# First experts of a two-layer mixture-of-experts kernel: output products as three products of split operands, written-out loop, two gather buffers

## The reference, cut to what matters

```python
B, L, D = (4, 1024, 256); F = 1024; E = 16        # here 2 x 1024 tokens, so capacity = 128
_, idx = jax.lax.top_k(logits.T, top_k)            # each expert takes its 128 best tokens
xe = xn[idx]
h = jnp.einsum('ecd,efd->ecf', xe, fc1_weight) + fc1_bias[:, None, :]
h = jax.nn.gelu(h, approximate=False)
y = jnp.einsum('ecf,edf->ecd', h, fc2_weight) + fc2_bias[:, None, :]
gates = jnp.take_along_axis(probs.T, idx, axis=1)
contrib = (y * gates[:, :, None]).reshape(-1, d)
output = jnp.zeros((n_tokens, d), dtype=x.dtype).at[flat_idx].add(contrib)
gate_sums = jnp.zeros((n_tokens, 1), dtype=x.dtype).at[flat_idx].add(gates.reshape(-1, 1))
```

## Time and profile before

| what | value |
|---|---|
| time of the kernel before, median of 3 runs | 859.65 us (858.2 to 859.97) |
| the profiled execution's own time | 855.36 us |
| its span on the core | 853.6 us |
| mean granted TensorE clock, share of full speed | 0.877 |
| PE busy | 681.3 us (80%) |
| DVE / ACT / POOL busy | 477.6 / 341.7 / 401.6 us |
| stage of the first experts, first transpose to last scatter's issue | 233.4 to 358.8 us |

### The profile page before, as it was taken

One profiled execution on the slowest core, in us unless ns is written; L12 is line 12 of the kernel. 1 busy time (PEld: TensorE's weight loads), 2 busy tenths in 40 slices (PEclk: granted clock), 3 DMA queues, 4 the chain that ended last, 5 costly groups with the idle time before them and its releaser, 6 DMA issues. The chain is left out here.

```text
span 853.6 us, 14267 instructions
## 1 busy us (share of the span) xinstructions
PE 681.3 (80%) x4385; PEld 624.7 (73%) x4386; DVE 477.6 (56%) x1023; ACT 341.7 (40%) x739; POOL 401.6 (47%) x515
## 2 busy tenths in 40 slices
PE   0767777710599999669999998996999999999980
PEld 0666667600499989656888877886899899999980
DVE  3353554368511111163988788974677864676740
ACT  1243435210033323224333343324766665667750
POOL 2132112000144455432565556643687766887883
PEclk9767585555699999869999999997999999999995
DMA  8961490040059998289010102007676564572221
GB/s 235 146 166 39 111 338 0 6 121 4 7 171 322 314 314 231 39 288 332 13 38 26 38 26 76 13 5 238 207 221 200 141 187 87 171 207 40 41 48 21
DMA packets 91760, 111.56 MB, mean 131 GB/s; under 512 B 9632, under 2 KB 80672, under 8 KB 91296
## 3 DMA queue, kind: packets, MB, share of 16 engines
q1 hardware_dynamic: 74032, 89.66, 34.4%
q0 software_dynamic: 11536, 14.30, 9.1%
q10 hardware_dynamic: 6112, 6.61, 2.3%
HBM read 93.84 MB, written 17.32 MB: 130 GB/s over the span
## 5 line engine op out<-in xcount | busy, mean ns | idle before, releaser
L1939 POOL DMA_INDIRECT out<-nyg,si x51 | 82.2, 1611 | 17.9 <-issue 17.9
L1538 POOL TENSOR_TENSOR hidl<-sums,hidh 128x512 fp32r<-128x512 f32 x40 | 52.2, 1305 | 76.4 <-ACT hidh L1726 76.4
L121 POOL TENSOR_TENSOR held<-ones 128x1 f32<-128x1 f32 x137 | 44.8, 327 | 90.1 <-DMA acc<-myg,si 34.2
L1358 POOL DMA_INDIRECT nG<-ytab,gi x54 | 77.4, 1434 | 16.3 <-issue 16.2
L2051 ACT ACTIVATE nh<-npH,c_sb 128x288 f32<-128x288 f32 x128 | 63.5, 501 | 45.4 <-PE npH L1992 44.8
L1851 DVE SCALAR_TENSOR_TENSOR xc<-pY,W,xc 128x264 f32<-128x264 f32 x160 | 67.3, 484 | 0.0
L1611 PE MATMUL pU<-xparts,gparts 128*128 128x512 f32 x240 | 65.3, 408 | 1.3 <-DVE xparts L1782 1.3
L1611 PE MATMUL pG<-xparts,gparts 128*128 128x512 f32 x240 | 63.1, 398 | 1.7 <-ACT sums L1711 1.7
L1104 PEld LDWEIGHTS mpH<-mXT,w_sb 128*128 128x128 f32 x512 | 61.2, 196 | 1.8 <-DVE mXT L1135 1.1
L1104 PE MATMUL mpH<-mXT,w_sb 128*128 128x128 f32 x512 | 61.5, 280 | 0.7 <-DVE mXT L1135 0.7
L1622 PE MATMUL pY<-dparts,hidh 128*128 128x264 f32 x320 | 60.4, 284 | 0.0
(11 more groups left out here) (412 smaller groups left out, 1857.3 us busy)
## 6 DMA issues: line engine op xcount, KB each, us to landing
w_sb<-in_w SPq DMA_DIRECT2D x32, 1024.0 KB, 8.4
w_sb<-in_v SPq DMA_DIRECT2D x30, 1024.0 KB, 8.9
bias_sb<-in_bias SPq DMA_DIRECT2D x4, 1024.0 KB, 14.7
gw<-in_wgate SPq DMA_DIRECT2D x17, 128.0 KB, 2.2
gw<-in_wup SPq DMA_DIRECT2D x17, 128.0 KB, 2.4
acc<-zrow SPq DMA_DIRECT2D x1, 2056.0 KB, 25.6
sums<-acc SPq DMA_DIRECT2D x4, 514.0 KB, 5.7
x_sb<-in_x SPq DMA_DIRECT2D x1, 2048.0 KB, 10.8
```

The source lines that it names most:

```text
L121: pool.tensor_tensor(held[:, n:n + 1], ones[:, 0:1], ones[:, 0:1], ALU.mult)
L1358: pool.indirect_dma_start(G[:, n], None, ytab, bass.IndirectOffsetOnAxis(ap=gi3[:, n:n + 1], axis=0)).then_inc(gathered, 16)
L1538: pool.tensor_tensor(hidl[:, s % 2], hid[:, s % 2], hidh[:, s % 2], ALU.subtract).then_inc(lo_ready, 1)
L1939: pool.indirect_dma_start(result, bass.IndirectOffsetOnAxis(ap=si3[:, n:n + 1], axis=0), yg[:, n], None, bounds_check=B * N - 1, oob_is_er ...
```

## The change

The function is replaced by straight code for all 16 blocks, with no loop.

- The output products take split operands: ACT rounds the hidden values `hT` to `hh` and the expert's second weights to `w2high`; DVE forms the rests `hl` and `w2low`; PE makes 24 products of 256 columns in fp32r instead of 8 in fp32. The first products stay plain fp32.
- PE runs one block behind: `first(j+1)`, `turn(j+2)`, `second(j)`. The bank of first products `pH` is doubled, and so are the split operands.
- The gathered rows have two buffers, and POOL issues the gather of block j+3 ahead of the scatter of block j.
- SP reloads a buffer once the block's first products are done and its second weights are split (`w_low`), no longer after its output products.
- DVE's order within a block is: outputs of block j-1, `low` of expert j+1 (128x2048), `column` of block j+2, and the rests of block j+1's hidden values in two halves.
- The stage ends with a wait for its last scatter.

```diff
@@ -991,172 +991,187 @@
-            def expert_phase(tag, src, width, dst, out_width, gidx, sidx, gates, from_row, b1t, b2t, w1t, w2t,
-                             experts, act_fn, counts):
...
-                            with eng.Fori(0, experts // RING) as r:
-                                for u in range(RING):
...
-                                for c in range(FC):
-                                    pe.wait_ge(gelu_done, j * FC + c + 1)
-                                    ins = pe.matmul(pY[:, 0:D], hT[:, c], w2_sb[:, u, c], start=(c == 0), stop=(c == FC - 1))
-                                ins.then_inc(fc2_done, 1)
...
-            expert_phase("m", table[0:B * N, :], ROW, acc0, D + 1, idx, idx, gtab, True, b1_sb, b2_sb, w1, w2,
-                         E0, ACT.Gelu, None)
+                G = sb("mG", [P, 2, ROW], into=ph)
+                XT = sb("mXT", [P, KD, P], into=ph)
+                hT = sb("mhT", [P, FC, P], into=ph)
+                hh = sb("mhh", [P, 2, FC, P], F32R, into=ph)
+                hl = sb("mhl", [P, 2, FC, P], F32R, into=ph)
+                w2high = sb("mw2h", [P, 2, FC, D], F32R, into=ph)
+                w2low = sb("mw2l", [P, 2, FC, D], F32R, into=ph)
+                yt = sb("myt", [P, D], into=ph)
+                yg = sb("myg", [P, D + 1], into=ph)
+                pX = ps("mpX", [P, 512], ph)
+                pH = ps("mpH", [P, 2, 2, 512], ph)
+                pY = ps("mpY", [P, 512], ph)
...
+                    @block.sync
+                    def _(sp):
+                        for e in range(E0 - RING):
+                            sp.wait_ge(fc1_done, 2 * e + 2)
+                            sp.wait_ge(w_low, e + 1)
+                            load_expert(sp, w1, w2, e + RING, e % RING)
+                    @block.gpsimd
+                    def _(pool):
+                        def gather(j):
+                            if j >= 1:
+                                pool.wait_ge(gathered, 16 * j)
+                            if j >= 2:
+                                pool.wait_ge(turned, j - 1)
+                                pool.wait_ge(xt_ready, j - 1)
                                 held_here(pool, 1)
+                            pool.tensor_copy(gi[:], idx[:, j:j + 1]).then_inc(gi_set, 1)
+                            pool.wait_ge(gi_set, j + 1)
+                            held_here(pool, 0)
+                            pool.indirect_dma_start(G[:, j % 2], None, table[0:B * N, :],
+                                                    bass.IndirectOffsetOnAxis(ap=gi[:], axis=0)).then_inc(gathered, 16)
+                        for j in range(3):
+                            gather(j)
+                        for j in range(E0):
+                            if j + 3 < E0:
+                                gather(j + 3)
+                            if j >= 1:
+                                pool.wait_ge(scattered, 16 * j)
                                 held_here(pool, 2)
+                            pool.tensor_copy(si[:], idx[:, j:j + 1]).then_inc(si_set, 1)
+                            pool.wait_ge(yg_ready, j + 1)
+                            pool.wait_ge(si_set, j + 1)
+                            held_here(pool, 3)
+                            pool.indirect_dma_start(acc0, bass.IndirectOffsetOnAxis(ap=si[:], axis=0), yg[:], None,
+                                                    compute_op=ALU.add).then_inc(scattered, 16)
+                        pool.wait_ge(scattered, 16 * E0)
+                        held_here(pool, 2)
+                    @block.tensor
+                    def _(pe):
+                        def turn(j):
+                            pe.wait_ge(gathered, 16 * (j + 1))
+                            if j >= 1:
+                                pe.wait_ge(xt_ready, j)
+                            for k in range(KD):
+                                ins = pe.transpose(pX[:, k * P:(k + 1) * P], G[:, j % 2, k * P:(k + 1) * P], ident[:])
+                            ins.then_inc(turned, 1)
+                        def first(j):
+                            pe.wait_ge(xt_ready, j + 1)
+                            pe.wait_ge(w_in[j % RING], 32 * (j // RING + 1))
+                            if j >= 2:
+                                pe.wait_ge(gelu_done, 2 * (j - 1))
+                            for c in range(FC):
                                 for k in range(KD):
+                                    ins = pe.matmul(pH[:, j % 2, c // HC, (c % HC) * P:(c % HC + 1) * P],
+                                                    w1_sb[:, j % RING, k, c * P:(c + 1) * P], XT[:, k], start=(k == 0), stop=(k == KD - 1))
+                                if c % HC == HC - 1:
+                                    ins.then_inc(fc1_done, 1)
+                        def second(j):
+                            pe.wait_ge(w_low, j + 1)
+                            if j >= 1:
+                                pe.wait_ge(y_read, j)
+                            for c in range(FC):
+                                if c % HC == 0:
+                                    pe.wait_ge(hl_ready, 2 * j + c // HC + 1)
+                                pe.matmul(pY[:, 0:D], hl[:, j % 2, c], w2high[:, j % 2, c], start=(c == 0), stop=False)
+                                pe.matmul(pY[:, 0:D], hh[:, j % 2, c], w2low[:, j % 2, c], start=False, stop=False)
+                                ins = pe.matmul(pY[:, 0:D], hh[:, j % 2, c], w2high[:, j % 2, c], start=False, stop=(c == FC - 1))
+                            ins.then_inc(fc2_done, 1)
+                        turn(0)
+                        first(0)
+                        turn(1)
+                        for j in range(E0):
+                            if j + 1 < E0:
+                                first(j + 1)
+                            if j + 2 < E0:
+                                turn(j + 2)
+                            second(j)
+                    @block.scalar
+                    def _(act):
+                        def high(e):
+                            act.wait_ge(w_in[e % RING], 32 * (e // RING + 1))
+                            if e >= 2:
+                                act.wait_ge(fc2_done, e - 1)
+                            act.activation(w2high[:, e % 2], w2_sb[:, e % RING], ACT.Copy).then_inc(w_high, 1)
+                        def hidden(j):
+                            for half in range(2):
+                                act.wait_ge(fc1_done, 2 * j + half + 1)
+                                if j >= 1:
+                                    act.wait_ge(hl_ready, 2 * (j - 1) + half + 1)
+                                for c in range(HC * half, HC * half + HC):
+                                    ins = act.activation(hT[:, c], pH[:, j % 2, half, (c % HC) * P:(c % HC + 1) * P], ACT.Gelu,
+                                                         bias=b1_sb[:, j, c:c + 1])
+                                ins.then_inc(gelu_done, 1)
+                                act.wait_ge(gelu_done, 2 * j + half + 1)
+                                if j >= 2:
+                                    act.wait_ge(fc2_done, j - 1)
+                                cs = slice(HC * half, HC * half + HC)
+                                act.activation(hh[:, j % 2, cs], hT[:, cs], ACT.Copy).then_inc(hh_ready, 1)
+                        high(0)
+                        hidden(0)
+                        for j in range(E0):
+                            if j + 1 < E0:
+                                high(j + 1)
+                                hidden(j + 1)
+                    @block.vector
+                    def _(dve):
+                        def column(j):
+                            dve.wait_ge(turned, j + 1)
+                            if j >= 1:
+                                dve.wait_ge(fc1_done, 2 * j)
+                            dve.tensor_scalar(gtab[:, j:j + 1], G[:, j % 2, D + j:D + j + 1], 1.0, None, ALU.mult)
+                            dve.tensor_copy(XT[:].rearrange("p k t -> p (k t)"), pX[:, 0:D]).then_inc(xt_ready, 1)
+                        def low(e):
+                            dve.wait_ge(w_high, e + 1)
+                            if e >= 2:
+                                dve.wait_ge(fc2_done, e - 1)
+                            dve.tensor_tensor(w2low[:, e % 2], w2_sb[:, e % RING], w2high[:, e % 2], ALU.subtract).then_inc(w_low, 1)
+                        def rest(j, half):
+                            dve.wait_ge(hh_ready, 2 * j + half + 1)
+                            cs = slice(HC * half, HC * half + HC)
+                            dve.tensor_tensor(hl[:, j % 2, cs], hT[:, cs], hh[:, j % 2, cs], ALU.subtract).then_inc(hl_ready, 1)
+                        def outputs(j):
+                            dve.wait_ge(fc2_done, j + 1)
+                            if j >= 1:
+                                dve.wait_ge(yg_ready, j)
```

(45 more changed lines are left out.)

128 lines of the change are left out of this document (removed).

## The result

The changed kernel takes 890.04 us in the median of 4 runs (886.61 to 895.15), the kernel before 858.92 (857.91 to 859.97): a ratio of 1.0367, 95% interval [1.0314, 1.042]. The forecast was slower, by 9.8 us; it is slower by 31, above the range. The profiled execution is the slowest, 895.15, with a span of 893.0.

The account below looks back on a forecast made before the run. PE's 7.24 us block was taken as the pace, covered by equally long DMA traffic; a scatter cycle of 8.5 us a block put PE's end at +7.8, the tail +2.0: 859.65 + 9.8 = 869.5 us, range 851 to 879.

Parts of the forecast that it names:

- PE's block: PE's time per block in the experts' stage: 7.24 us falls to 6.60 through shorter output products, a gain of 0.64.
- Work added: Per block ACT comes to 5.7 us and DVE to some 5.2, both fitting in PE's 6.60 on their own.
- The wait that matters: DVE's outputs wait for the previous block's scatter; low, column and rests queue behind, then PE and SP's next load.
- POOL against DVE: A GpSimd instruction starting during DVE's 2.29 us subtraction stands still until it ends; held takes 2.21, a scatter's issue 3.58.
- The start: First blocks of the stage: scatter 0 and the next gather come late, PE waits about 3 us, first(4) at 265.0, not 261.8.
- The cycle: Multiplication, low, held and scatter wait on each other: period 3.5 + 5.0 = 8.5 us a block; chance 0.66.
- L: A scatter's time to landing within the period: taken as 5.0 us, bounds 3.9 (quiet) and 6.0 (median under full DMA).
- The sum: Blocks 4 to 11 at 8.5 us, three at 7.0; PE ends at 363.4 (+7.8), tail +2.0, together +9.8 us.
- Costed at nothing: Three items put at zero: loops written out, the wait for the stage's last scatter, and earlier loads.
- Clock: A clock cost of PE's pauses was left out: PE paused 1.67 of 2 us at 306 and stayed at 1.00.
- PE keeps the pace: Faster rival: held or the scatter's issue gets in ahead of low, blocks of 6.6 us, 849.8 us; chance 0.21.
- The turns of the queues: By the skill page, DMA engines alternate queues packet by packet, so scatters skip whole-load waits: L near 3.9, period 7.4.

Follow-up runs that it names:

- e4: Changed kernel with the weight loads of experts 4 to 15 cut to 64 columns of one row per tile; 849.96 us, ratio 0.996 to the kernel before.
- e3: Changed kernel with a small POOL copy behind each scatter that the weight load waits for, so the scatter is issued first; 863.77 us, ratio 1.010 to the kernel before.
- e10: Changed kernel with each gather issued one block earlier and each weight load waiting for the issue of scatter e-2; 872.44 us, ratio 1.017 to the kernel before.

## Why the prediction was wrong

*PE's block*: forecast 6.60, measured 6.67 where nothing holds PE (e4). Right. *Work added*: `low` 2.28, rests 0.68, rounding 1.91 and 0.63 against 2.3, 0.71, 1.91 and 0.63. Right. *The wait that matters* and *POOL against DVE*: right, 62.2 us in 15 pieces, and `held` at 2.17.

*The start*: first(4) at 264.36, forecast 265.0, and that is luck. The first scatter got in ahead of low(2) (250.30 against 251.01), so the gather of block 4 went out at 253.89 instead of 257.3; but it stood 0.5 us behind a load (253.38) and took 7.3 us to land, where the forecast had 4.7. The cycle begins with the second scatter.

*The cycle* is the step that failed, in the size of its terms. The period was to be 3.5 + L with L = 5.0. Measured are 2.9 and 7.7: from first(4) to first(12) it is (349.80 - 264.36) / 8 = 10.68 a block instead of 8.5, and 8 x 2.18 = 17.4 us of the miss. The 3.5 was too high, as `held` ends with `low` and doesn't stand behind it. For L I argued that the load "no longer fills" a period, as if it lay somewhere in it by chance. It has a fixed place: SP and POOL wait for the same end of `low`, and the load is first each time. e3 and e10 show that this order made the difference. The upper bound of 6.0 was a median of another order, in which single scatters took up to 7.7; the 10.3 that I read as a scatter's is a read by the next stage.

*The sum*: the last three intervals took 8.15 each instead of 7.0 (374.25 - 349.80), +3.5; from first(15) to the last scatter's issue 16.02 instead of 12.9, +3.1; the start -0.6. With 17.4 that is 23.4: 390.27 against a forecast of 366.9.

*Costed at nothing*: the wait for the last scatter, as the next stage waited for it too. From that scatter's issue to the next stage's first read it is 6.9 to 7.1 us in the changed kernel and every version of it, 5.7 before: 1.4 us that the sum lacks.

*Clock*: "not in the sum" was wrong as a fact. Output products that began after a wait took 318.02 - 312.90 = 5.12 us, 2.95 without one (292.92 to 295.87 in e3). In the cycle the slack hid it, as DVE still waited for scatters behind these products (62.2 us); in e3's long blocks it adds some 1.4 us (16 x 0.09).

*Rivals*: "PE keeps the pace" named the state that e4 is in, and the point of decision, who comes first, was right; that it has to be won anew after each late landing was not seen.

*The turns of the queues.* The Trainium skill, page "DMA: Bandwidth & Descriptors", section "Queues, rings and completion order", has an engine take turns between queues packet by packet, a packet there being a run of some 9 to 17 descriptors that is drained whole. An estimate from that page, with a row of 4 KB as one descriptor: the first tile's 256 rows are 16 for each of 16 engines, about one such packet. So the forecast's "L near 3.9" took a single row for a turn, and the page leaves room for a scatter that waits for the whole tile. The trace agrees as far as it goes: the scatter of 304.03 has nothing moving until the first tile is through, and beside the second tile both queues move; its L is 7.7.

## What to carry to other kernels

Ask of each long instruction not only what it blocks but what its end sets free at the same moment: the two transfers released together here went out in the same order each time, the bulk one first, and an engine waited for the one behind it. An in-order engine that waits for a transfer and then starts the next one can have two steady states; work out the period of the slow one and see whether it is longer than the bound that you hope for. Before shortening an engine's work, look at whether its share is full together with another's: here PE's 0.57 us a block was had only in e4, without the loads; no version with them got it over the stage.

## What was unexpected of the hardware

While the load's first tile (1 MB in 4 KB packets) passes, POOL's queue moves nothing: no packet from 305.0 to 308.5, with the scatter issued at 304.03 and its first packet 4.8 us later, where e3's scatter of 290.71 had its first packet 2.2 us after the issue (a packet of the profile is one row here). Cut into four transfers with 1 KB packets, the same bytes let it through earlier (landing 5.8 instead of 7.7).

PE's granted clock stayed 1.00 while it stood idle for 2.5 us, and was 0.50, the lower level of 1.2 GHz, from 302.4, just after it resumed, to 305.8 (e3); in the changed kernel it fell at 311.0, in a wait of 3.94 that ended at 312.55, and stayed 0.50 to 317.8. After the 1.67 us pause of the kernel before it was 1.00 in every stretch to 314.
